# Softmax attention's scores, maximum items and masks issued as four column tiles of 32

## The chip, the cores and the metric

The kernel runs on one core of one Trainium2 chip. The metric is the device time of one execution in microseconds (us). Three runs of the kernel before took 1463.82, 1464.60 and 1467.52 us; the median is 1464.6 us.

## What is computed

Four layers run one after the other on an input `x` of shape (4, 1024, 128), each followed by `x = layernorm(x + layer(x))`: softmax attention, a gated feed-forward layer with ternary weights, linear attention with decay, and a mixture of experts. The change is in the first. It has 16 heads of 8 dimensions:

```
q, k, v = split(x @ w_qkv)                     # per head: 1024 x 8
scores  = q @ k.T / sqrt(8), keys after the query masked with -inf
out     = softmax(scores) @ v
return concat(out) @ w_out
```

## The kernel before

**Units.** A unit is one batch entry and four heads; there are 16 (`NU`). The program of each engine is written out for units 0 and 1, loops over units 2 to 13 with two units in the loop's body (`with_loop(eng, 1, NU // 2 - 1, ...)`, six passes), and is written out again for units 14 and 15. Engines meet by semaphores alone, and each executes its program in the order written.

**The inputs of a product.** q and k are split into three bf16 parts each, which are stacked along the partitions in `sq` and `sk`: 96 rows (`MROW`) give the scores of a query and a key, and three more rows (`PARTS`) in `sq` hold the negated maximum of each query, against rows of ones in `sk`.

**Two passes over the scores.** TensorE first computes the maxima's scores: `item(u, p, k)` writes 128 queries x up to 512 keys for two or four heads into one of two pairs of PSUM banks (`pair[k % 2]`), at line 1206, and adds the causal mask to its last 128 columns with a product of the identity and `mask_qk`, at line 1209. VectorE reduces every item to one maximum per query and head (`top`, line 1367). There are 21 items a unit, numbered 0 to 20, 80 matmuls with their 32 masks. An item waits for the reduction of the item two before it (`s_itc`). When all are reduced, `chain` on VectorE splits the maxima into three parts, `turn_max` on TensorE transposes them (line 1220, eight matmuls with 12 columns of weights), VectorE copies them out (line 1394), and DMAs write them to `sq`.

The second pass, `scores` (line 1231), writes keys x queries with the maximum already taken off, in 36 steps of one bank each (48 matmuls), into three banks in turn. ScalarE takes the exponential of each (line 1320) into one of 12 slots of `pe_`; GpSimd zeroes the triangle above the diagonal in the blocks on it (`triangle`, line 1488).

**The products with v** (`times_v`, line 1256) come in ten groups a unit (`GROUPS`, numbered 0 to 9), after the exponentials (and triangles) of the group are there. They are float32 with 32 columns of weights (8 dimensions, a one for the sum, padding), one head per group of 32 partitions of `pv_bank`: four matmuls that differ in the columns of the array that they use. The profile shows two records for each, one for each pass of a float32 product. VectorE then transposes and normalises (`norm`, lines 1402 to 1414).

**The order on TensorE.** Unit u interleaves its own scores and products with the items of unit u + 1: for each group g, two steps of scores, an item, two steps, an item, then the products of group g - 1, then what is left of the items (`PER_GROUP`). `turn_max(u + 1)` comes after group 7. The items 0 to 2 of unit u + 2 come in group 9. The items of unit 0 are done ahead of all, and unit 15 has none beside it.

Of the kernel before, what the change touches and what calls it, by code (L numbers as in the profile page):

```python
# [21 lines left out]
P = 128  # L22
# [10 lines left out]
PARTS = 3  # L33
SROWS = PARTS * PARTS * D0
MROW = 96
# [76 lines left out]
def program(nc, a, out):  # L112
    with ExitStack() as ctx:
        def sb(name, shape, dt=F32):
            return ctx.enter_context(nc.sbuf_tensor(name, shape, dt))
# [14 lines left out]
        identb = sb("identb", [P, P], BF16)  # L130
        mask_qk = sb("mask_qk", [P, P], BF16)
# [30 lines left out]
        sq = [view([P, HQ, T], BF16) for p in range(2)]  # L162
        sk = [view([P, HQ, T], BF16) for p in range(2)]
# [1004 lines left out]
        def _(e):  # L1168
# [21 lines left out]
            e.wait_ge(s_r1, 4 * B)  # L1190
            e.wait_ge(s_v, 2 * B)

            def item(u, p, k, i=None):

                qt, hs, k0, n = ITEMS[k]
                if k == 0:
                    e.wait_ge(s_st[p][0], 16 * 8 * (i + 1))
                if k == HALF_ITEM:
                    e.wait_ge(s_st[p][1], 16 * 8 * (i + 1))
                if not (isinstance(u, int) and u == 0 and k < 2):  # L1200
                    e.wait_ge(s_itc, NI * u + k - 1)
                for at, h in enumerate(hs):
                    col = at * n if len(hs) == 4 else at * 512
                    dst = pair[k % 2].rearrange("p a c -> p (a c)")[:, col:col + n]
                    diag = k0 + n > qt * P
                    ins = nc.tensor.matmul(dst, sq[p][0:MROW, h, qt * P:(qt + 1) * P], sk[p][0:MROW, h, k0:k0 + n],  # L1206
                                           start=True, stop=not diag, skip_group_check=True)
                    if diag:
                        ins = nc.tensor.matmul(dst[:, n - P:n], identb[:, :], mask_qk[:, :],  # L1209
                                               start=False, stop=True, skip_group_check=True)  # L1210
                ins.then_inc(s_it, 1)

            def turn_max(u):
# [10 lines left out]
            def scores(u, p, steps):  # L1224

                for s in steps:
                    if not (isinstance(u, int) and u == 0 and s < NBANK):
                        e.wait_ge(s_exp, NS * u + s - NBANK + 1)
                    bank = score[s % NBANK]
                    for h, kt, q0, n, at in STEPS[s]:  # L1230
                        ins = nc.tensor.matmul(bank[:, at:at + n], sk[p][0:MROW + PARTS, h, kt * P:(kt + 1) * P],  # L1231
                                               sq[p][0:MROW + PARTS, h, q0:q0 + n], start=True, stop=True,
                                               skip_group_check=True)
                    ins.then_inc(s_qk, 1)

            def times_v(u, p, g):
# [27 lines left out]
            for k in range(NI - 1):  # L1264
                item(0, 0, k, 0)
            turn_max(0)

            def unit(u, p, first, last, i):

                for g in range(NG):  # L1270
                    if g == 0:
                        e.wait_ge(s_mrow, 16 * HQ * (u + 1))
                    steps = range(FIRST_STEP[g], FIRST_STEP[g] + len(GROUPS[g][1]))
                    items = max_work(g, first, isinstance(u, int) and u == NU - 2, last)

                    def next_item():
                        ahead, k = items.pop(0)
                        item(u + ahead, p if ahead == 2 else 1 - p, k, i + 1 if ahead == 2 else i + p)
                    for n in range(2):
                        scores(u, p, steps[2 * n:2 * n + 2])  # L1280
                        if items:
                            next_item()
                    if g or not first:
                        times_v(*((u, p, g - 1) if g else (u - 1, 1 - p, NG - 1)))
                    while items:
                        next_item()
                    if not last and g == CHAIN_SLOT:
                        turn_max(u + 1)
# [300 lines left out]
```

## Time and profile before

| | |
|---|---|
| median of the runs | 1464.6 us |
| the profiled execution: its own time, its span | 1472.18 us, 1470.5 us |
| PE (TensorE matmul), busy in the span | 1281.0 us, 87%, 10608 records |
| PEld (weight loads) | 738.8 us, 10609 records |
| DVE (VectorE) | 979.5 us, 67% |
| ACT (ScalarE) | 642.1 us, 44% |
| POOL (GpSimd) | 536.1 us, 36% |
| mean granted TensorE clock | 0.944 |

The profile is one execution; its terms are compared with its own time, and the median is that of other executions. "Busy" is the time in which at least one instruction of the engine is under way; matmuls overlap one another, and their ends are modelled, so differences between starts say more than durations. The softmax attention's two passes run from 43.8 us (first item) to 579.2 us (last product with v) after the span's start; the scores start at 76.1 us. Records of LDWEIGHTS (PEld) and MATMUL (PE) are separate; every matmul of the program has both.

### The profile page before, as it was taken

To read this page: it belongs to the slowest core of one execution; us is meant where nothing else is said; L and a number is where in the kernel's file an instruction comes from. 1 tells how busy PE (TensorE), PEld (TensorE's weight loads), DVE (VectorE), ACT (ScalarE), POOL (GpSimd) and SP (SyncE) were. 2 spreads that over 40 slices of the span, in tenths; PEclk is the share of its full clock that TensorE was granted. 3 is DMA by queue.
4 is the path that set the end of the run, shared out by engine and by line. 5 is a ranking of instruction groups with operands and counts; after the bars stand their busy time and mean duration, and the time that the engine had idled before them with its cause. 6 is when DMAs were issued, how large, how long until landed. Compare 5 with 4: busy or idle time off the path is not lost. (4 is left out here: it accounts for less than half of the span.)

```text
span 1470.5 us, 33772 instructions
## 1 busy us (share of the span) xinstructions
PE 1281.0 (87%) x10608; PEld 738.8 (50%) x10609; DVE 979.5 (67%) x2119; ACT 642.1 (44%) x1280; POOL 536.1 (36%) x615
## 2 busy tenths in 40 slices
PE   6699999999999996799999999999999977299990
PEld 4233333334333332356556565746565645299980
DVE  6868888877888881247584848485857556366656
ACT  4155556565556655242433334242524231155553
POOL 7112232323232322005261616253444434244456
PEclk9589999999999999799999999999999988599995
DMA  6452111111111110321121303030303050232215
GB/s 190 114 179 54 38 39 36 45 46 48 41 38 36 37 39 21 100 54 40 46 67 30 82 27 86 14 98 14 98 12 87 2 156 2 73 96 65 65 55 173
DMA packets 91756, 93.59 MB, mean 64 GB/s; under 512 B 16816, under 2 KB 77104, under 8 KB 91568
## 3 DMA queue, kind: packets, MB, share of 16 engines
q1 hardware_dynamic: 73872, 74.91, 18.7%
q0 software_dynamic: 9184, 13.39, 3.1%
q10 hardware_dynamic: 8640, 4.53, 1.1%
q8 instruction: 33, 0.54, 0.2%
q14 instruction: 27, 0.22, 0.1%
HBM read 49.84 MB, written 22.63 MB: 49 GB/s over the span
## 5 line engine op out<-in xcount | busy, mean ns | idle before, releaser
L1320 ACT ACTIVATE arena<-banks 128x512 f32<-128x512 f32 x576 | 302.4, 600 | 231.9 <-PE banks L1231 231.3
L1367 DVE TENSOR_REDUCE arena<-banks 128x4 f32<-128x512 f32 (+3 forms) x336 | 347.7, 1057 | 77.3 <-PE banks L1209 71.9
L1206 PE MATMUL banks<-arena 96*128 96x512 bf16 (+3 forms) x768 | 207.8, 344 | 25.7 <-DVE arena L1367 19.0
L424 PE MATMUL banks<-arena,h 128*128 128x512 f32 x512 | 226.7, 593 | 2.4 <-DVEq L369 1.0
L1231 PE MATMUL banks<-arena 99*128 99x512 bf16 (+3 forms) x768 | 176.7, 330 | 16.3 <-ACT arena L1320 11.3
L1488 POOL TENSOR_SCALAR_AFFINE_SELECT arena<-arena 128x512 f32<-128x512 f32 x128 | 79.9, 636 | 241.5 <-ACT arena L1320 241.4
L1256 PE MATMUL banks<-arena 128*32 128x512 f32 (+3 forms) x1536 | 156.8, 496 | 4.4 <-POOL arena L1488 2.7
L424 PEld LDWEIGHTS banks<-arena,h 128*128 128x128 f32 x512 | 94.7, 190 | 110.0 <-issue 105.0
L570 ACT ACTIVATE arena<-banks,sh 128x512 f32<-128x512 f32 x64 | 44.0, 687 | 214.4 <-PE banks L424 214.4
L1206 PEld LDWEIGHTS banks<-arena 96*128 96x128 bf16 x768 | 71.6, 101 | 125.8 <-DVE arena L1367 82.9
L440 POOL TENSOR_TENSOR arena<-arena 128x4 f32<-128x4 f32 x24 | 24.4, 1019 | 278.1 <-DVE arena L438 278.1
L1231 PEld LDWEIGHTS banks<-arena 99*128 99x128 bf16 x768 | 60.2, 98 | 123.2 <-ACT arena L1320 88.7
L1496 POOL DMA_DIRECT2D att_t<-arena x124 | 62.5, 506 | 142.2 <-DVE arena L1414 131.3
L609 POOL TENSOR_TENSOR arena<-arena,qdec 128x512 f32<-128x512 f32 x64 | 87.6, 1391 | 64.1 <-DVE arena L513 42.8
L950 ACT ACTIVATE arena<-banks,b_in 128x128 f32<-128x128 f32 x288 | 82.2, 368 | 63.4 <-PE banks L932 60.2
L983 POOL DMA_INDIRECT best<-arena x72 | 71.8, 998 | 89.2 <-DVE arena L970 48.2
L1209 PE MATMUL banks<-mask_qk,identb 128*128 128x128 bf16 x512 | 102.8, 228 | 0.0
L558 POOL TENSOR_TENSOR arena<-arena,kdec 128x512 f32<-128x512 f32 x64 | 84.5, 1345 | 35.7 <-ACT arena L549 20.7
L684 DVE SCALAR_TENSOR_TENSOR arena<-arena,bdec,banks 128x128 f32<-128x128 f32 x256 | 69.0, 343 | 30.5 <-PE banks L671 30.5
L424 PE MATMUL banks<-h,arena 128*128 x576 | 81.0, 284 | 3.5 <-ACT arena L950 2.4
L932 PE MATMUL banks<-arena 128*128 128x128 f32 x576 | 79.4, 282 | 1.7 <-DVE arena L963 1.7
L823 POOL DMA_INDIRECT rows<-arena x64 | 62.7, 979 | 49.5 <-DVE arena L797 22.6
(162 smaller groups left out, 1947.9 us busy)
## 6 DMA issues: line engine op xcount, KB each, us to landing
arena<-arena SPq DMA_DIRECT2D x160, 128.0 KB, 2.3
arena<-k_parts SPq DMA_DIRECT2D x96, 96.0 KB
arena<-rows SPq DMA_DIRECT2D x72, 65.0 KB
arena<-q_parts SPq DMA_DIRECT2D x64, 64.0 KB
arena<-best SPq DMA_DIRECT2D x16, 256.0 KB, 4.6
k_parts<-arena SPq DMA_DIRECT2D x24, 128.0 KB, 3.0
arena<-q_parts SPq DMA_DIRECT2D x32, 96.0 KB
q_parts<-arena POOLq DMA_DIRECT2D x18, 128.0 KB, 3.0
```

What stands on the lines that cost most here:

```text
L424: ins = nc.tensor.matmul(dst, l, r, start=(n == 0), stop=(n == len(pairs) - 1), skip_group_check=True)
L558: lambda: nc.gpsimd.tensor_tensor(v_dec[:, n % 2, kp, :, :].rearrange("p g (i d) -> p g i d", i=4), v_nat[:, n, 2 * kp:2 * kp + 2, :].rear ...
L609: lambda: nc.gpsimd.tensor_tensor(q_dec[:, n % 2, 4 * kp:4 * kp + 4, :, :], q_all[:, 4 * kp:4 * kp + 4, n * P:(n + 1) * P].rearrange("p i ...
L932: ins = nc.tensor.matmul(banks[:, 2 + k % 2, m * P:(m + 1) * P], w_now[:, k % 4, m * P:(m + 1) * P], x_gT[:, k % 4, :], start=True, stop=T ...
L950: ins = nc.scalar.activation(h_g[:, k % 2, m * P:(m + 1) * P], banks[:, 2 + k % 2, m * P:(m + 1) * P], ACT.Gelu, bias=b_in[:, bass.ds(x, 1 ...
L1206: ins = nc.tensor.matmul(dst, sq[p][0:MROW, h, qt * P:(qt + 1) * P], sk[p][0:MROW, h, k0:k0 + n], start=True, stop=not diag, skip_group_ch ...
L1209: ins = nc.tensor.matmul(dst[:, n - P:n], identb[:, :], mask_qk[:, :], start=False, stop=True, skip_group_check=True)
L1231: ins = nc.tensor.matmul(bank[:, at:at + n], sk[p][0:MROW + PARTS, h, kt * P:(kt + 1) * P], sq[p][0:MROW + PARTS, h, q0:q0 + n], start=Tru ...
L1256: done.append(nc.tensor.matmul(pv_bank[32 * h:32 * h + 32, lo:lo + n], va[p][:, kt, h, :], pe_[:, s % NSLOT, at:at + n], start=(g in (0, 3 ...
L1320: nc.scalar.activation(pe_[:, s % NSLOT, :], score[s % NBANK], ACT.Exp, scale=SCALE0)\
L1367: nc.vector.tensor_reduce(mx[:, 1 if k0 else 0, qt, hs[0]:hs[-1] + 1], src, AX.X, ALU.max)\
L1488: ins = nc.gpsimd.affine_select(out=v, in_=v, compare_op=ALU.is_ge, fill=0.0, base=0, pattern=[[0, v.shape[1]], [1, P]], channel_multiplie ...
```

## The change

Each matmul of line 1206 (items), line 1209 (masks) and line 1231 (scores) had 128 columns of weights and wrote 128 partitions. It becomes four matmuls, one after the other, with 32 columns of the weights each, the same streamed operand, and 32 partitions of the output each. The semaphore is incremented by the last of the four. Nothing else changes: the order of the work, the waits, the banks, the other engines' programs and the transposes of `turn_max` stay.

```diff
+            def columns4(dst, lhs, rhs, start, stop):
+
+                for c in range(0, P, 32):
+                    ins = nc.tensor.matmul(dst[c:c + 32, :], lhs[:, c:c + 32], rhs, start=start, stop=stop,
+                                           skip_group_check=True)
+                return ins
+
             def item(u, p, k, i=None):
...
-                    ins = nc.tensor.matmul(dst, sq[p][0:MROW, h, qt * P:(qt + 1) * P], sk[p][0:MROW, h, k0:k0 + n],
-                                           start=True, stop=not diag, skip_group_check=True)
+                    ins = columns4(dst, sq[p][0:MROW, h, qt * P:(qt + 1) * P], sk[p][0:MROW, h, k0:k0 + n],
+                                   True, not diag)
                     if diag:
-                        ins = nc.tensor.matmul(dst[:, n - P:n], identb[:, :], mask_qk[:, :],
-                                               start=False, stop=True, skip_group_check=True)
+                        ins = columns4(dst[:, n - P:n], identb, mask_qk[:, :], False, True)
                 ins.then_inc(s_it, 1)
...
                     for h, kt, q0, n, at in STEPS[s]:
-                        ins = nc.tensor.matmul(bank[:, at:at + n], sk[p][0:MROW + PARTS, h, kt * P:(kt + 1) * P],
-                                               sq[p][0:MROW + PARTS, h, q0:q0 + n], start=True, stop=True,
-                                               skip_group_check=True)
+                        ins = columns4(bank[:, at:at + n], sk[p][0:MROW + PARTS, h, kt * P:(kt + 1) * P],
+                                       sq[p][0:MROW + PARTS, h, q0:q0 + n], True, True)
                     ins.then_inc(s_qk, 1)
```

## Rows read from the trace of the kernel before

**Rows 1.** Busy time and records of each engine in two units; columns as named.

```profile
core 0: us, PE busy (x) PEld busy (x) DVE busy (x) ACT busy (x) POOL busy (x), PEclk, DMA share, GB/s
...
139.00:202.00 63.00, 58.73 (x463) 24.25 (x462) 51.57 (x71) 37.61 (x72) 18.88 (x34) 1.00 0.18 44
```

**Rows 2.** Timeline of DVE; start, length, what, [idle before <-releaser].

```profile
441.66 2.36 DVE L1367 TENSOR_REDUCE arena<-banks 128x4 f32<-128x1024 f32 x2 [0.46 <-PE banks L1209]
...
452.47 1.23 DVE L1367 TENSOR_REDUCE arena<-banks 128x2 f32<-128x1024 f32 x1 [0.35 <-PE banks L1209]
...
455.73 0.68 DVE L1394 COPY arena<-banks 12x1024 bf16<-12x1024 bf16 x1 [0.87 <-PE banks L1220]
459.13 1.29 DVE L1367 TENSOR_REDUCE arena<-banks 128x4 f32<-128x512 f32 x2 [2.72 <-PE banks L1209]
461.10 0.69 DVE L1367 TENSOR_REDUCE arena<-banks 128x2 f32<-128x512 f32 x1 [0.68 <-PE banks L1209]
461.98 1.92 DVE L1367 TENSOR_REDUCE arena<-banks 128x2 f32<-128x768 f32 x2 [0.19 <-PE banks L1209]
```

**Rows 3.** Timeline of PE around three groups of products with v.

```profile
407.64 1.07 PE L1256 MATMUL banks<-arena 128*32 128x384 f32 x16
408.65 0.60 PE L1231 MATMUL banks<-arena 99*128 99x512 bf16 x2
...
410.73 0.64 PE L1256 MATMUL banks<-arena 128*32 128x256 f32 x8
411.30 0.60 PE L1231 MATMUL banks<-arena 99*128 99x512 bf16 x2
...
413.00 0.22 PE L1209 MATMUL banks<-mask_qk,identb 128*128 128x128 bf16 x1
413.15 1.07 PE L1256 MATMUL banks<-arena 128*32 128x512 f32 x8
414.15 0.60 PE L1231 MATMUL banks<-arena 99*128 99x512 bf16 x2
```

**Rows 4.** Timeline of PE from the transposes of the maxima to the next unit.

```profile
423.30 0.61 PE L1220 MATMUL banks<-identb,arena 128*12 128x128 bf16 x8 [0.18 <-DVE arena L1384]
423.84 0.83 PE L1231 MATMUL banks<-arena 99*128 99x384 bf16 x6
...
426.76 0.22 PE L1206 MATMUL banks<-arena 96*128 96x128 bf16 x1
426.82 0.22 PE L1209 MATMUL banks<-mask_qk,identb 128*128 128x128 bf16 x1
...
427.85 1.07 PE L1256 MATMUL banks<-arena 128*32 128x384 f32 x16
...
429.20 0.59 PE L1231 MATMUL banks<-arena 99*128 99x512 bf16 x2
```

**Rows 5.** Timeline of PE in unit 15, which has no items beside it.

```profile
568.34 1.06 PE L1256 MATMUL banks<-arena 128*32 128x512 f32 x8
...
570.74 1.07 PE L1256 MATMUL banks<-arena 128*32 128x512 f32 x8
```

**Rows 6.** Timeline of PE, the window from 413.14 to 413.17 us alone.

```profile
413.15 0.64 PE L1256 MATMUL banks<-arena 128*32 128x512 f32 x4
```

**Rows 7.** DMA by queue: 139 to 202 us, all queues of 202 to 515, 582 to 720; an issue of the page.

```profile
q8 instruction: 4, 0.07, 0.5%
...
q1 hardware_dynamic: 13039, 11.49, 13.1%
q0 software_dynamic: 2502, 1.29, 2.0%
...
q8 instruction: 7, 0.11, 0.3%
...
arena<-arena SPq DMA_DIRECT2D x160, 128.0 KB, 2.3
```

**Rows 8.** Timeline of PE in the linear attention.

```profile
681.26 1.11 PE L671 MATMUL banks<-arena 64*64 64x64 f32 x64
682.19 1.05 PE L621 MATMUL banks<-arena 64*64 64x256 f32 x16
```

## The prediction

> **What bounds the kernel now.** The change touches only TensorE's program in the softmax attention, so I read the stretches of that part first, by the table of windows. In two whole units (63 us) PE is busy for 58.7 us, DVE for 51.6, ACT for 37.6 [rows 1]. PE is the fullest, but a busy PE contains modelled ends, and 51.6 of 63 is no idle DVE either. So next I read DVE's timeline over one unit, some 31.5 us [rows 2]. DVE has work back to back except in six places, where it waits for TensorE: 0.46, 0.35, 0.87, 2.72, 0.68 and 0.19 us, 5.3 us in all. Between them DVE sets the pace: whatever PE gains there, PE waits longer for DVE. The reader is to see here that a faster PE shortens a unit only by what it takes out of these six gaps.
>
> **What a switch of tile shape costs.** Third, PE's own timeline. The last mask before a group of products with v starts at 413.00 and the products at 413.15 [rows 3]; a mask of 128 columns otherwise takes 0.06 us (426.76 to 426.82 [rows 4]). So going in costs 0.09 us. For the way out I compare groups of two lengths [rows 3]: the groups x16 (384 and then 128 columns) and x8 of 512 columns, each in two passes, last 1.01 and 1.00 us until the next score starts, the group of 256 columns 0.57 us. Half the columns, 0.43 us less: so 0.86 us is streaming and about 0.14 us is fixed. It is paid once, however many rounds of four tiles there are (four in x16, two in x8), so the rounds themselves add nothing. I read it as waiting for the array to empty (some 0.09 again) and the first 32-column weights, that nothing covers. That it is the shape and not bf16 against float32 is seen at turn_max: eight 12-column transposes in bf16 take 0.54 us until a full-width bf16 score starts (423.30 to 423.84 [rows 4]), where eight of 128 columns would be 0.06 x 8 = 0.44 by the masks' pace: 0.09 or 0.10 again, with no change of type.
>
> **The change, part by part.** Removed: per unit 10 groups x (0.09 + 0.14) = 2.3 us, and about 0.2 at the transposes: 2.5 us of PE time, 40 us in 16 units, the most that the change could bring if PE alone were the bound. The parts that lie in DVE's gaps:
> 1. Gap before items 0 and 2, 3 (2.72, 0.68, 0.19): PE's path runs from the transposes over the scores of group 8 and the products of groups 7 and 8. The products of group 8 start at 427.85 [rows 4] although PE has nothing else to do by then: they wait for GpSimd's triangle, which comes from an exponential of group 8, and this moves only by the 0.09 after the transposes. So of this path the 0.09 and the 0.09 to 0.1 behind group 8 remain: 0.18 us, in 14 units: 2.5 us. (What is won at group 7 is lost again in the wait for the triangle.)
> 2. Gap before item 12 (0.46): it hangs on item 11, which DVE itself released, and one group of products in between: 0.23 less 0.03 for the weights and the stagger below: 0.2 us, in 15 units: 3.0 us.
> 3. Gap before item 20 (0.35): from item 12 on PE runs nearly without a wait through four groups of products, 4 x 0.23 = 0.9 us, more than the gap: it closes, 0.35 x 15 = 5.2 us. The rest becomes PE's wait for DVE.
> 4. Gap before the copy of the transposed maxima (0.87): chain of DVE's own results; nothing.
> 5. After the last item (unit 14's end and unit 15) PE and ACT take turns: four scores and a group of products each 2.40 us (568.34 to 570.74 [rows 5]), of which the two switches are 0.2; 13 groups, some waiting for the triangle: I take 2.3 us.
> Sum of the gain: 2.5 + 3.0 + 5.2 + 2.3 = 13.0 us.
>
> Added: every matmul of scores, items and masks becomes four with 32 columns of weights. Four tiles side by side start within one window of 0.03 us [rows 6], so the last ends about 0.02 us after the first. A round costs one matmul's streaming, if its weights load under the round before. In a stream nothing is added. Where PE comes out of a wait, the last tile's semaphore is 0.02 later and the first weights are seen: 0.04 us. In the gaps above that is already off; the 20 items of unit 0 ahead of the loop, where nothing switches, give a loss: 20 x 0.04 = 0.8 us.
>
> Also added: instructions. A unit has 128 matmuls that become 512, so 768 more records with their weight loads, on (463 + 462) / 2 = 463 now [rows 1]. The loop body holds two units. While it is first run, 4 instruction packets of queue q8 arrive for 925 records (I take q8 for PE's: no other engine has so many instructions); from 202 to 515 us there is none: the body stays in PE's instruction memory [rows 7]. Afterwards the body is 925 + 1536 = 2461 records, at 925 / 4 = 231 a packet and with the uncounted register instructions staying as they are, 10 to 11 packets. The most that this trace shows to stay is the later loop's, 7 packets fetched between 582 and 720 [rows 7]. So 10 may not stay. Fetched in order they are harmless: one per 6 us. But at each of the 5 jumps back to the top (6 passes) the top may be missing. Price of one: from nothing (it stays, or PE's queue covers it) to 2.3 us, what a small transfer of this kernel takes from issue to landing (the 128 KB moves in [rows 7]). PE's sequencer is at the jump when the triangle lets group 8 go, at 427.85, and the next unit's scores start at 429.20 [rows 4], 1.3 us later. What shows is 2.3 - 1.3 = 1.0 at the upper end; I take 0.8 us, 5 x 0.8 = 4 us, bounds 0 and 5 x 2.3 = 11.5 us.
>
> The Trainium skill speaks to this place ("Runtime: NRT & Kernel Launch", section "Instruction fetch mechanics"): PE's instruction memory holds 2048 instructions in blocks of 256, and a taken branch to a block that isn't there stalls for a fetch. The rows agree as far as they go (231 counted records a packet, no fetch during the small loop); none shows a stall. By it the body would be over the limit and the 4 us would be sure to be paid at least in part; without it they could be nothing.
>
> Sum: -13.0 + 0.8 + 4 = -8.2 us. The profiled execution took 1472.2 us for a span of 1470.5, 7.6 us above the median of 1464.6; the terms are differences, so I take them from the median: 1456.4.
>
> **Rivals.**
> A. The body stays or the jumps are covered, and PE's gain reaches DVE a little more than I count: 1464.6 - 13 = 1452, down to 1447 where group 7's gain counts as well (0.2 x 14 = 3 us). For it: the six gaps are all PE's. Against it: packets.
> B. Jumps cost double (two packets at each, or 2.3 us all exposed): 11.5 us instead of 4, total -0.7: 1464, no change. For it: nothing covers PE at this place, DVE is idle there too. Against it: PE's queue holds some work.
> C. Slower: a round of four bf16 tiles doesn't keep a full-width matmul's pace, because the weights of 32 columns don't hide. Place: each of 128 rounds a unit. The nearest row: the fixed part at the products has 0.03 us more at its start than one switch. At 0.027 a round, 3.5 us a unit against 2.5 won; in the stretches that end in DVE's gaps lie about 90 rounds, 2.4 us against the 0.73 won there, less what the DVE-bound waits swallow, about 1 us a unit: 15 us, 1480. It decides from about 10 ns a round. Against it: four rounds cost no more overhead than two [rows 3], and 16 rounds of four 64-column float32 tiles take 0.93 us (681.26 to 682.19 [rows 8]), 0.058 a round against 0.054 of streaming (0.43 us for twice 256 columns, scaled to 64): 4 ns more, with a change of operands in it. For it: no row has bf16 tiles at the short rounds of 128 columns, where eight instructions must issue in 0.055 us.
> The Trainium skill speaks for C ("TensorEngine Tiling (Array Packing)", "Performance Considerations" and "Restrictions"): column tiling excludes the fast weight load. Whether the slower loads hide under a 128-column bf16 round no row shows. By this rule alone the time would go towards 1480.
> D. The switch isn't what the 0.09 is (say, each group waits so for its semaphore in any case): nothing is won, the added costs stay: 1464.6 + 4.8 = 1469. Against it: the same 0.09 at the transposes.
>
> **How the numbers follow.** No change that this kernel's measurement can tell is within 0.3%, 4.4 us: 1460.2 to 1469.0. Forecast (1452 to 1460) 0.45; A 0.18; B 0.18; C 0.13; D 0.06. Faster: 0.45 + 0.18 = 0.63; same: most of B and half of D, 0.20; slower: C, part of B and D, 0.17. A range of 1447 to 1467 leaves out C, a part of D, and gains beyond A.
>
> **What will show it.** PE's timeline: the next score starts 0.86 us after a group x8 of 512 columns began, not 1.00; a round of four 512-column tiles takes 0.216 us, one of 128 columns 0.056 (C: 0.08 or more). DVE's gap before item 20 gone, that before item 12 near 0.25, the 0.87 as it was, a unit near 30.8 us. In the DMA view instruction packets between 202 and 515 us, about 10 per 62 us if the body doesn't stay, and every second unit a PE gap of about a microsecond after item 2, with the cause "issue". The prediction is wrong if rounds are slower than full-width matmuls, if the jump costs 2 us or more in the open, or if DVE's gaps stay as they are.

## The result and the profile after

The changed kernel takes 1475.45 us (median of four runs, 1474.34 to 1478.62); the kernel before took 1464.21 us beside it. The ratio is 1.0076, 95% interval 1.0053 to 1.0099: slower by 11 us, where 8 us faster was forecast. The profiled execution took 1478.62 us, the longest of the four, and has a span of 1477.0 us.

I read the same views as before. First the windows of PE and DVE: the two units ahead of the first jump, and then the 250 us in which four of the jumps lie (the columns are those of [rows 1]).

```profile
139.00:202.00 63.00, 57.22 (x1300) 29.46 (x1292) 52.14 (x71) 39.42 (x75) 19.99 (x36) 1.00 0.18 46
202.00:265.00 63.00, 54.68 (x1123) 26.78 (x1124) 50.64 (x69) 34.80 (x67) 17.21 (x33) 0.95 0.16 45
265.00:515.00 250.00, 217.28 (x4564) 110.01 (x4566) 188.62 (x255) 139.17 (x264) 68.90 (x124) 0.93 0.16 43
```

In the first two units DVE has more to do in 63 us than in [rows 1] (52.1 against 51.6) and PE, with 1300 records for 463, is busy for 1.5 us less: the work runs faster. From 202 us on both are busy for less, and the granted clock is below 1. So the loss isn't in the column tiles; it begins with the loop's second pass. The pace of a unit, further down, says the same.

DVE's timeline over one unit without a jump, the rows that answer to [rows 2]:

```profile
437.50 0.68 DVE L1399 COPY arena<-banks 12x1024 bf16<-12x1024 bf16 x1 [0.87 <-PE banks L1226]
440.60 1.29 DVE L1372 TENSOR_REDUCE arena<-banks 128x4 f32<-128x512 f32 x2 [2.42 <-PE banks L1196]
442.69 0.69 DVE L1372 TENSOR_REDUCE arena<-banks 128x2 f32<-128x512 f32 x1 [0.80 <-PE banks L1196]
443.56 1.84 DVE L1372 TENSOR_REDUCE arena<-banks 128x2 f32<-128x768 f32 x2 [0.19 <-PE banks L1196]
...
454.75 2.35 DVE L1372 TENSOR_REDUCE arena<-banks 128x4 f32<-128x1024 f32 x2 [0.23 <-PE banks L1196]
```

2.72 became 2.42, 0.68 became 0.80, 0.46 became 0.23, the 0.87 is as it was; the 0.35 ahead of item 20 is gone.

PE's timeline around products with v and over the jump, the rows that answer to [rows 3] and [rows 4]:

```profile
401.90 1.03 PE L1261 MATMUL banks<-arena 128*32 128x512 f32 x8
402.77 0.67 PE L1196 MATMUL banks<-arena 99*32 99x256 bf16 x20
...
404.53 1.07 PE L1261 MATMUL banks<-arena 128*32 128x384 f32 x16 [0.35 <-POOL arena L1493]
405.42 0.29 PE L1196 MATMUL banks<-arena 96*32 96x256 bf16 x4
405.53 0.24 PE L1196 MATMUL banks<-mask_qk,identb 128*32 128x128 bf16 x4
405.59 0.29 PE L1196 MATMUL banks<-arena 96*32 96x256 bf16 x4
405.70 0.24 PE L1196 MATMUL banks<-mask_qk,identb 128*32 128x128 bf16 x4
409.08 0.78 PE L1196 MATMUL banks<-arena 99*32 99x512 bf16 x12 [3.14 <-issue]
...
412.22 0.51 PE L1196 MATMUL banks<-arena 96*32 96x384 bf16 x4 [1.55 <-issue]
```

The next score starts 0.87 us after a group x8 of 512 columns (1.00 before), and a round of four tiles takes 0.11 us with 256 columns (405.42 to 405.53) and 0.06 with 128 (405.53 to 405.59), the pace of full width (0.06 by [rows 4]; 365.06 to 365.17 us with 256 columns in full_straight, a kernel of the next section): those steps of the prediction hold. But at 405.9, after item 2 and ahead of the next unit's first score, where the loop jumps to its top, PE stops for 3.14 us. The first jump's stop, at 203.5, is 3.37 us long. Both are far over the 0.8 us that I took and over the 2.3 us of my bound. After it PE runs at half the clock (the same columns as above; 0.51 is the mean of the two levels, almost all at 1.2 GHz):

```profile
206.00:212.90 6.90, 5.88 (x80) 2.69 (x84) 2.67 (x4) 2.17 (x4) 0.64 (x1) 0.51 0.12 35
410.70:417.60 6.90, 5.38 (x80) 2.82 (x84) 4.41 (x6) 1.86 (x5) 0.63 (x1) 0.51 0.01 2
437.00:451.00 14.00, 12.33 (x335) 7.10 (x332) 10.09 (x14) 7.70 (x15) 4.16 (x8) 1.00 0.19 52
```

The DMA queues, 139 to 202 us and then 202 to 515 us, answer to [rows 7]:

```profile
q8 instruction: 11, 0.18, 1.2%
...
q8 instruction: 56, 0.92, 1.3%
```

11 packets in the loop's first pass, and 12 in each pass after it (56 in 313 us, of which a pass takes 67): the body doesn't stay in PE's instruction memory.

The same queue tells what each stop at a jump consists of. At 405.94 PE stops; a packet of 16 KB starts at 406.02 and ends at 407.48; PE goes on at 409.08. So it is at all five jumps: the packet starts 0.08 to 0.27 us after PE has stopped and takes 0.9 to 1.6 us, and PE goes on 1.6 to 1.7 us after its end. Ahead of the second stop, of 1.55 us, a packet ends at 410.83, and PE goes on at 412.22, 1.4 us later. (These are the starts and durations of the trace's q8 packets.)

For the pace of a unit I use a row of DVE's chain that occurs once a unit (the CAST of `chain`), asked from 190 to 500 us: its count, and its first and last start. Before, then after:

```profile
L1382 DVE CAST arena<-arena x10: 197/199/199, 200.6 to 486.2; 128x32 bf16<-128x32 f32 x10
```

```profile
L1387 DVE CAST arena<-arena x9: 195/195/195, 197.1 to 466.8; 128x32 bf16<-128x32 f32 x9
```

Before, (486.2 - 200.6) / 9 = 31.73 us a unit. After, a unit without a jump takes 30.6 (197.1 less 166.5, the start of the one ahead), and one with a jump 35.9 to 36.7. One unit without a jump took 31.9. There PE waited for a DMA, and the granted clock was 0.50 from 380.0 to 383.4 us:

```profile
379.49 2.29 PE L1196 MATMUL banks<-arena 96*32 96x512 bf16 x32 [1.41 <-DMA arena<-q_parts]
```

### The profile page after: what moved, and what is told of

Read it like the earlier page. It is cut to its first block and busy times, and to the rows that moved or that the text cites. A ratio compares the mean times of both kernels' runs of the same rounds, so it can differ in the third digit from the quotient of the medians.

```text
span 1477.0 us, 46060 instructions
## 1 busy us (share of the span) xinstructions
PE 1265.1 (86%) x16752; PEld 773.2 (52%) x16753; DVE 974.2 (66%) x2119; ACT 644.3 (44%) x1280; POOL 532.3 (36%) x615
## 3 DMA queue, kind: packets, MB, share of 16 engines
q1 hardware_dynamic: 73872, 74.91, 18.4%
## 5 line engine op out<-in xcount | busy, mean ns | idle before, releaser
L1196 PE MATMUL banks<-arena 99*32 99x512 bf16 (+7 forms) x6144 | 357.6, 344 | 62.3 <-issue 17.5
L1196 PEld LDWEIGHTS banks<-arena 96*32 96x32 bf16 (+1 forms) x6144 | 159.8, 99 | 238.1 <-DVE arena L1372 71.4
L1196 PE MATMUL banks<-mask_qk,identb 128*32 128x128 bf16 x2048 | 110.4, 234 | 0.2
L558 POOL TENSOR_TENSOR arena<-arena,kdec 128x512 f32<-128x512 f32 x64 | 80.9, 1290 | 30.1 <-PE banks L546 25.8
L680 ACT COPY arena<-banks 128x512 f32<-128x512 f32 x64 | 34.4, 590 | 89.7 <-PE banks L671 89.7
L932 PEld LDWEIGHTS banks<-arena 128*128 128x128 f32 x576 | 71.5, 195 | 2.5 <-issue 2.3
```

Of the source, the lines that this page charges most:

```text
L558: lambda: nc.gpsimd.tensor_tensor(v_dec[:, n % 2, kp, :, :].rearrange("p g (i d) -> p g i d", i=4), v_nat[:, n, 2 * kp:2 * kp + 2, :].rear ...
L932: ins = nc.tensor.matmul(banks[:, 2 + k % 2, m * P:(m + 1) * P], w_now[:, k % 4, m * P:(m + 1) * P], x_gT[:, k % 4, :], start=True, stop=T ...
L1196: ins = nc.tensor.matmul(dst[c:c + 32, :], lhs[:, c:c + 32], rhs, start=start, stop=stop, skip_group_check=True)
```

## The experiments

Twelve runs follow, in four groups. Each group has its own runs of the kernel before, to which its ratios refer: 1464.33 us for the first four kernels, 1468.29 for the next three, 1471.11 for pause_54, pause_20, straight_again and after_again, 1468.33 for pause_31. Between groups it is the ratios that compare, not the medians.

**The loop taken away, with and without column tiles.** In TensorE's program alone all 16 units are written out, so that nothing jumps back. The same edit in both kernels; `full` is the kernel before, `cols` the changed one.

```diff
-            units(e, unit)
+            for u in range(NU):
+                unit(u, u % 2, u == 0, u == NU - 1, u // 2)
```

> The changed kernel (all in four column tiles) with TensorE's attention program written out for all 16 units, no loop; the other engines keep their loops. Theory J (the loss is the 5 jumps back to the top of a body that no longer stays in TensorE's instruction memory, each 3.1 + 1.6 us of stall and a half clock after it): a unit of the changed kernel without a jump repeats in 30.6 us, one with a jump in 36.7, so 5 x 6.1 = 30 us come back: 1475.4 - 30 = 1445 us, 0.987 of the kernel before. Rival R (the four-tile rounds or the number of instructions are the cost, wherever they are): written out, the same instructions run, 1475 us; a straight program even fetches more packets.

> The kernel before (full-width matmuls) with TensorE's attention program written out in the same way; its waits then compare with constants, without register instructions. Theory J: its body of two units stayed in memory, its jumps cost nothing: 1464 us, ratio 1.000. Rival W (any loop or the register instructions at the waits cost TensorE time): faster, by as much as a good part of what the written-out changed kernel wins, 1450 or less.

cols_straight took 1448.34 us, ratio 0.989 (0.9868 to 0.991), full_straight 1463.94 us, 0.9997 (0.9985 to 1.0008). Their chain rows, cols_straight first:

```profile
L1388 DVE CAST arena<-arena x10: 195/195/197, 195.5 to 470.8; 128x32 bf16<-128x32 f32 x10
```

```profile
L1383 DVE CAST arena<-arena x10: 196/198/199, 200.5 to 485.5; 128x32 bf16<-128x32 f32 x10
```

30.59 and 31.67 us a unit. The column tiles bring 16 us, and all that the changed kernel loses, 27 us between ratios 1.0076 and 0.989, comes with the loop. That the waits now compare with constants gains nothing by itself: full_straight has that too. Nor is it the fetching as such: cols_straight fetches 49 packets from 202 to 515 us, about as many as the changed kernel's 56, but in order, and hides all of them.

**Half as many jumps.** The loop's body holds four units, with two jumps instead of five. At full width the body then holds 2 x 925 = 1850 counted records, where two units of column tiles have 2461 by the prediction's count.

```diff
-            units(e, unit)
+            for u in range(2):
+                unit(u, u % 2, u == 0, False, 0)
+            with_loop(e, 0, (NU // 2 - 2) // 2,
+                      lambda j: [unit(2 * (2 * j + m) + p, p, False, False, 2 * j + m)
+                                 for m in range(1, 3) for p in range(2)])
+            for u in range(NU - 2, NU):
+                unit(u, u % 2, False, u == NU - 1, u // 2)
```

> The kernel before (full-width matmuls) with four units in TensorE's loop body instead of two: 3 passes, 2 jumps. Twice the 4 packets and more of the two-unit body, so about as many as didn't stay in the changed kernel. Theory J: the long body doesn't stay, 2 jumps of 5 to 6 us each, though not one matmul is tiled: 1464 + 11 = 1475 us, instruction packets all through the attention, two half-clock stretches. Rival R (tiles are the cost): 1464 us.

> The changed kernel with four units in TensorE's loop body: 3 passes, 2 jumps instead of 5. Theory J: three jumps fewer, 1475.4 - 3 x 6.1 = 1457 us. Rival R: 1475 us.

full_4units took 1475.1 us, ratio 1.0075 (1.0058 to 1.0092): with no column tile in it the kernel before becomes as slow as the changed one, by two jumps. In the table of PE's waits, 200 to 480 us (total, times, longest):

```profile
PE banks L1231 <- issue: 6.1, 2, 3.1
```

The kernel before has no such row. The two units with a jump took 37.3 and 36.5 us, 5.5 and 4.8 over the others, for stops of 3.0 and 3.1. The body of four full-width units, too, is fetched anew (23 packets from 202 to 515 us, 10 of them in the pass between the two jumps, where the kernel before has none): 1850 counted records, with the uncounted ones beside them, are already more than stays.

cols_4units took 1465.13 us, 0.9998 (0.9983 to 1.0012). Three jumps fewer won back 10 us against the changed kernel's 1475.45, where 18 were expected (1457 us). Its two jumps don't account for the whole distance to cols_straight, (1465.13 - 1448.34) / 2 = 8.4 us each: by the trace each is 6.5 to 6.7 us (37.1 and 37.2 us for 30.5 and 30.6). Most of the rest, 0.1 to 0.9 us a unit, lies in units without a jump. In five of them PE stops, again with the cause "issue", for 0.17 to 0.62 us, 1.8 us in all, and each time it goes on 1.3 to 1.6 us after the end of a 16 KB packet, as after the changed kernel's second stop. So here fetching in order is not always hidden; 2 us more in those units have no row.

**One of the two groups of matmuls alone, no loop.** `wide` issues one full-width matmul. In cols_items_only the scores stay full width, in cols_scores_only the items and masks do.

```diff
-                        ins = columns4(bank[:, at:at + n], sk[p]...
+                        ins = wide(bank[:, at:at + n], sk[p]...
```

> Written out like cols_straight, but only items and masks in four column tiles; the scores go back to full width. Theory S (the gain is the switches of tile shape that go away): the order of a unit has 20 changes between full width and 32 columns in the kernel before, none with all in tiles, and 32 here, since the scores now stand between items and products. The 20 were worth 16 us (1464 to 1448), 0.05 us each; 12 more than before at 0.05 to 0.1 us, 15 units: 1473 to 1482 us, slower than both. Rival T (the tiled matmuls are themselves quicker, by their weight loads or their concurrency): most matmuls are tiled, so most of the gain stays, about 1454 us.

> Written out, only the scores in four column tiles, items and masks at full width. Theory S: 36 changes of shape a unit, 16 more than before: 1476 to 1488 us. Rival T: a third of the tiled matmuls, a third of the gain, about 1459 us.

They took 1482.45 us, ratio 1.0102 (1.0075 to 1.0128), and 1488.72 us, 1.0143 (1.0116 to 1.017), each less than 1 us over its expected range, beside a kernel before that was itself 4 us slower than in the first group. Chain rows in this order:

```profile
L1392 DVE CAST arena<-arena x10: 197/197/197, 205.3 to 497.2; 128x32 bf16<-128x32 f32 x10
```

```profile
L1392 DVE CAST arena<-arena x9: 195/195/198, 205.5 to 467.6; 128x32 bf16<-128x32 f32 x9
```

32.43 and 32.76 us a unit. Half the change makes the kernel slower although no round is slower, since scores and items alternate: counted in the traces, TensorE's tile shape changes 0 times a unit in cols_straight, 20 in full_straight, 32 and 36 here. The units take 30.59, 31.67, 32.43 and 32.76: over cols_straight 0.054, 0.058 and 0.060 us a change. On PE's own timeline a change takes more. First cols_items_only, where two full-width scores of 512 columns stand between items in tiles, all bf16, then full_straight, where nothing changes:

```profile
373.91 0.60 PE L1202 MATMUL banks<-arena 99*128 99x512 bf16 x2
374.45 0.35 PE L1196 MATMUL banks<-arena 96*32 96x384 bf16 x4
```

```profile
365.23 0.59 PE L1231 MATMUL banks<-arena 99*128 99x512 bf16 x2
365.67 0.33 PE L1206 MATMUL banks<-arena 96*128 96x384 bf16 x1
```

0.54 us for 0.44: the change takes 0.10 us of PE, and a unit pays a little over half of it, since much of PE's time lies under DVE's. The number of changes orders all four kernels, and that is what the whole change wins; whether each kind of change costs exactly the same isn't shown.

**The blocks shifted.** 90 increments of an unused semaphore at the start of PE's program move every later instruction against the blocks in which the memory is filled. The second stop after a jump (1.55 us above) would be a block's edge soon behind the jump's target.

```diff
+            for _pad in range(90):
+                e.sem_inc(s_hold, 1)
```

> The changed kernel with its loop of two units (5 jumps), and 90 semaphore increments that nobody waits for at the very start of TensorE's program, while it waits for its inputs. They move the loop's top by 90 instructions, from near the end of a fetched block (TensorE stops a second time some 75 instructions after the top) to near the start of the next. Theory J2 (the first stall is the fetch of the block with the top, the second is the fetch of the block after it, which begins only when the first is there): the second stall (1.6 us) goes, the half clock after it gets shorter, 5 x 2 = 10 us: 1465 us. Rival K (each jump costs its 6 us wherever the top lies, for instance because the clock falls): 1475 us.

It took 1487.83 us, 1.0131 (1.0103 to 1.0159): by the ratios 8 us more, not 10 less, than the changed kernel. The increments themselves were hidden only in part: they take 13.6 us of PE's sequencer at the start, 0.151 us each, and the first product with v starts at 95.1 us for 87.2, 7.9 us later. The row of PE's sequencer (number, then first and last start):

```profile
L1170 PEldq EVENT_SEMAPHORE  x90: 51/51/51, 1.0 to 14.6; - x90
```

From there on the trace gains on the changed kernel's: its 15 units from the first chain to the last take 490.2 us for 493.8. At the jumps there is one stop now, but 3.2 to 3.7 us long:

```profile
PE banks L1198 <- issue: 13.7, 4, 3.7
```

The five units with a jump took 35.2 to 36.5 us, on average 36.0 instead of 36.4. The expected 2 us a jump did not come: it is 0.4. The expectation took a second stop at every jump, but the changed kernel has it at one of five (at two of five when it ran again, below), and the first stop is longer here instead (13.7 / 4 = 3.4 us a jump, as much as the changed kernel's 16.5 / 5 = 3.3 with both). That no second stop shows at five jumps fits the idea that it hangs on where the blocks lie, but with so few it isn't shown. And stops of 3.3 to 3.4 us don't explain a price of 5.5 to 5.8. So I looked at the half clock.

**A stop without a missing packet.** cols_straight with N increments ahead of units 4, 6, 8, 10 and 12, where the changed kernel jumps. All packets still come in order.

```diff
             for u in range(NU):
+                if u in (4, 6, 8, 10, 12):
+                    for _pad in range(N):
+                        e.sem_inc(s_hold, 1)
                 unit(u, u % 2, u == 0, u == NU - 1, u // 2)
```

> cols_straight (all tiles, no loop in TensorE's attention) with 54 semaphore increments that nobody waits for, before units 4, 6, 8, 10 and 12: the five places of the jumps. 90 of them took 7.9 us in cols_shifted, so 54 take 4.8 us, which is how long after group 8's products the next unit's scores started at a jump. No packet is missing here. Theory J3 (a jump costs what any stop of TensorE of 3.4 us at this place costs: the 3.4, and a half clock after it, 5.3 to 6 us in all; fetching itself has no further price): 1448.3 + 5 x 5.5 = 1476 us, half clock after each stop. Rival F (the fetch costs more than the stop, through slower issue or DMA after the jump): 1448.3 + 5 x 3.4 = 1465 us.

> The same with 20 increments, 1.8 us. Theory Q (TensorE's queue covers 1.3 us at this place, as predicted): about 0.5 us of stop remain, clock stays up: 1448.3 + 5 x 0.5 = 1451 us. Rival: nothing is covered, 1448.3 + 5 x 1.8 = 1457 us.

> The version with no loop, as pause_54 and pause_20, with 31 increments ahead of units 4, 6, 8, 10 and 12: at the 0.151 us that they stood apart there, 4.7 us of PE's sequencer, of which some 0.8 us were covered in pause_20. So PE should stop for 3.1 to 3.9 us at five places, as long as it stops at a jump of the changed kernel, with every instruction packet fetched in order. Theory (a stop brings half the clock after it, and that is the rest of a jump's price beside the missing packets): each place costs the stop and 1.3 to 2 us more, 5.0 to 5.9 us in all, so 25 to 30 us over the version without increments, beside a jump's 5.3 to 6.1. Rival (a bare stop costs itself, and the second stop behind a jump is the missing next packet's alone): 3.1 to 3.9 a place, 16 to 20 us in all, and no half clock after it.

Beside the first two of them the two kernels to be compared ran once more:

> cols_straight again on this chip, to stand beside the two runs with pauses: 1448 us by its first runs.

> The changed kernel again on this chip, to stand beside the runs with pauses: 1475 us by its first runs.

| kernel | median us | ratio (95%) | a stop, us | each place costs, us |
|---|---|---|---|---|
| straight_again | 1453.01 | 0.9887 (0.9856 to 0.9919) | none | |
| pause_20 | 1468.57 | 1.0 (0.9984 to 1.0016) | 2.2 | 3.3 |
| pause_31 | 1480.77 | 1.0083 (1.0067 to 1.01) | 3.9 | 5.8 |
| after_again (five jumps) | 1482.69 | 1.0097 (1.0065 to 1.0129) | 3.7 | 5.8 |
| pause_54 | 1500.47 | 1.0217 (1.0185 to 1.025) | 7.5 | 9.4 |

The kernels that ran again took 5 and 7 us more than in their first group, as the kernel before did, and their ratios are the same within the intervals. A stop is the total of the row "issue" in PE's waits from 200 to 480 us by the number of places in that window (both stops of a jump together for after_again, 18.4 / 5). A place costs what the units with it took over the others, on average. The rows are these; pause_20, pause_31, pause_54 (four of its places lie in the window), and that of the changed kernel's first profile:

```profile
PE banks L1196 <- issue: 10.9, 5, 2.2
```

```profile
PE banks L1196 <- issue: 19.4, 5, 4.0
```

```profile
PE banks L1196 <- issue: 29.8, 4, 7.6
```

```profile
PE banks L1196 <- issue: 16.5, 6, 3.4
```

Two expectations failed. pause_54 was to take 1476 us and took 1500: I had taken 7.9 / 90 = 0.088 us for an increment from cols_shifted, where 5.7 of the 13.6 us were hidden, but they stand 0.151 us apart, there as here, so that it stopped for 7.5 us, not as long as a jump. pause_20 was to take 1451, or 1457 if nothing is covered, and took 1469: it stopped for 2.2 us instead of 0.5 to 1.8, and half clock followed at four of its five places. pause_31 has the right length, and it is also the price of a jump. Its timeline of PE at one place, and the window behind another:

```profile
405.45 1.12 PE L1196 MATMUL banks<-arena 99*32 99x512 bf16 x12 [3.88 <-issue]
```

```profile
204.40:211.30 6.90, 6.70 (x97) 3.62 (x101) 3.67 (x4) 2.17 (x4) 0.64 (x1) 0.51 0.01 2
```

A stop of 3.9 us that has nothing to do with fetching brings the same half clock (at four of the five places the last packet had ended 3 us or more before PE went on, at one 1.65 us). By its chain rows the five places cost (498.5 - 194.3) - (470.8 - 195.5) = 28.9 us:

```profile
L1391 DVE CAST arena<-arena x10: 196/196/197, 194.3 to 498.5; 128x32 bf16<-128x32 f32 x10
```

So 5.8 us each, 3.9 of it the stop and 1.9 what follows it, which the trace shows as PE at 1.2 GHz for 3.4 us at two places (they cost 5.2 and 5.5 us) and for 6.8 us at three (6.2 each). The rival, that a bare stop costs itself alone, gives 19 us and falls. Within pause_31 the places with 3.4 us of half clock cost 1.3 and 1.6 us beyond their stop, those with 6.8 us 2.3. Where in pause_20 the clock stayed full after the stop (one of five places), that place cost 2.4 us, close to the stop's 2.2; the four with half clock behind them cost 3.2 to 3.8.

## Why the prediction was wrong

**The failed step** is the price of the jump: "What shows is 2.3 - 1.3 = 1.0 at the upper end; I take 0.8 us, 5 x 0.8 = 4 us, bounds 0 and 5 x 2.3 = 11.5 us." The mechanism came as told in its first half: the body didn't stay, 11 to 12 packets a pass, and a gap with the cause "issue" after item 2. Its size was wrong by a factor of seven, and the truth lay outside the bounds: 27 us between the ratios of the changed kernel and cols_straight, 29.7 us between the medians of after_again and straight_again, 5.4 to 5.9 a jump. Three things in it:

- The fetch. I took 2.3 us for it, from data transfers [rows 7], less 1.3 us for what lies ahead in PE's queue, and so expected a stop of about 1 us. The five first stops are 2.7 to 3.4 us: longer than the transfer with no cover taken off. The packets say why: nothing of the transfer lay under PE's work, since the packet started only once PE had stopped (0.08 to 0.27 us later), and to its 0.9 to 1.6 us come 1.6 to 1.7 us from its end until PE goes on. What the sequencer does ahead of the packet's start no run shows.
- In some jumps (one in five in the profiled execution) a second stop of 1.55 us follows. Its packet had ended 1.4 us before PE went on, which fits a next block that isn't there either. Rival B said "two packets at each, or 2.3 us all exposed": both at once and more.
- After the stop the clock is halved, for 6.8 to 10.2 us. No term and no rival had this. It is 1.9 us a place in pause_31; in the changed kernel the five jumps cost 5 x 5.8 = 29 us, of which 16.5 are stops, so that 12.5 lie behind them, 2.5 a jump. That all of the 2.5 is the clock isn't shown: 6.8 us of half clock were worth 2.3 in pause_31.

The prediction's own sign of being wrong came, "if the jump costs 2 us or more in the open". Rival B (the jumps cost double) had the right side and not the size: 11.5 us at most. What came was B's bound two and a half times over.

**The gain was in the right places and a little larger.** Forecast 13.0 us; by the ratios 0.9997 and 0.989 it is 15.7 us. DVE's groups of reductions, idle time before them in 12 units (busy and mean, then idle), full_straight and then cols_straight:

```profile
L1368 DVE TENSOR_REDUCE arena<-banks 128x2 f32<-128x1024 f32 x145 | 172.4, 1203 | 7.6 <-PE banks L1209 4.6
...
L1368 DVE TENSOR_REDUCE arena<-banks 128x2 f32<-128x512 f32 x24 | 16.5, 686 | 8.2 <-PE banks L1209 8.2
L1368 DVE TENSOR_REDUCE arena<-banks 128x4 f32<-128x512 f32 x24 | 16.4, 682 | 32.6 <-PE banks L1209 32.6
L1368 DVE TENSOR_REDUCE arena<-banks 128x4 f32<-128x1024 f32 x12 | 14.7, 1224 | 5.5 <-PE banks L1209 5.5
```

```profile
L1373 DVE TENSOR_REDUCE arena<-banks 128x2 f32<-128x1024 f32 x144 | 170.0, 1199 | 1.6
...
L1373 DVE TENSOR_REDUCE arena<-banks 128x2 f32<-128x512 f32 x24 | 16.5, 686 | 9.6 <-PE banks L1196 9.6
L1373 DVE TENSOR_REDUCE arena<-banks 128x4 f32<-128x512 f32 x24 | 16.4, 682 | 29.1 <-PE banks L1196 29.1
L1373 DVE TENSOR_REDUCE arena<-banks 128x4 f32<-128x1024 f32 x12 | 14.7, 1224 | 2.7 <-PE banks L1196 2.7
```

- Gaps before items 0, 2 and 3: (32.6 - 29.1 + 8.2 - 9.6) / 12 = 0.175 us a unit, 0.18 forecast. As told, what is won at group 7 is lost in the wait for the triangle (still 0.35 us at 404.53 above).
- Gap before item 12: (5.5 - 2.7) / 12 = 0.23, 0.2 forecast.
- The reductions of 1024 elements, item 20 among them: (7.6 - 1.6) / 12 = 0.50, 0.35 forecast. Term 3 was too small: beside the gap that I listed, PE's gain also closes small idle pieces among the others.
- The copy's gap: no gain from the tiles (9.5 us in both), as said.
- Together 0.9 us a unit of 31.67 - 30.59 = 1.08; reductions 4 ns shorter, twelve a unit, are 0.05 more. 0.1 us is in no row.
- The removed PE time was counted as 10 groups and the transposes besides. The trace has 20 changes of shape, not 22: the transposes follow a group of products (422.05 and 423.30 us in the kernel before), which already has 32 columns. This touches the upper limit of 40 us alone, no term of the sum.
- The tail: from the last chain to the last product with v 29.7 us became 28.6, 1.1 for 2.3 forecast. A turn of four scores and a group takes 2.19 (554.48 to 556.67 us in cols_straight) for 2.40 [rows 5], as told; fewer turns than I took decide it. In the sum of the gain this shortfall and the excess of term 3 (0.15 x 15 = 2.2 us) partly cancel.
- The start: unit 0's first chain is 1.0 us later (70.8 for 69.8), 0.8 forecast, but between executions of the same kernel it varies by as much (70.9 and 69.3 us in the changed one). From the first chain to the second 36.0 us became 33.2, for which no term stands; much of that may be the clock (half until 87.4 us in full_straight, until 80.6 in cols_straight) and no gain of the tiles, see the last section.

The sum with the measured terms is -15.7 + 27 = +11.3 us, the result; it must be, as both terms are taken from ratios to the same kernel. The traces give the second term independently: the five jumps of the changed kernel cost 28.9 us over its other units.

**Rivals A, C and D.** A asked for covered jumps and falls. C, slower rounds, falls: full width's pace at 128, 256 and 512 columns (0.06, 0.11 and 0.21 us, the last from 376.11 to 376.32 in the changed kernel), and cols_straight is the fastest kernel. The Trainium skill ("TensorEngine Tiling (Array Packing)", section "Restrictions") says that column tiling disables the fast weight load, which spoke for C. No cost of it shows here: with 1292 weight loads in 63 us where there were 462, a 128-column round of four bf16 tiles still takes 0.06 us. D falls by cols_straight itself and by the two half changes. The Trainium skill's "Runtime: NRT & Kernel Launch", "Instruction fetch mechanics", says that a taken branch to a block that isn't there stalls, and the traces agree: 2.7 to 4.3 us at each such jump. Its limit of 2048 instructions, in blocks of 256, is eight blocks; the traces agree as far as they go, with a loop of 7 packets that stays [rows 7] and bodies of 10 and 12 that don't. I weighed this rule as to whether the price is paid and took the price from a data transfer; that is the error.

## What to carry to other kernels

A change that multiplies instructions is first to be checked against what a loop's body holds: here a body that stays costs nothing at its jumps, one that doesn't costs 4.8 to 6.7 us at each, and the same body written out without a jump costs nothing again, since in order the fetches hide (in cols_straight; in the loop of cols_4units not quite). TensorE's tile shape costs 0.06 us of a unit's time at each change, so it pays to have one shape all through (-16 us) and costs to have it in one half alone (ratios 1.0102 and 1.0143). A stop of TensorE is to be priced at more than itself: one of 3.9 us cost 5.8 here. The version to use is cols_straight: 0.989 of the time before.

## What the runs showed of the hardware

- A jump whose target isn't in PE's instruction memory: 2.7 to 4.3 us of stop (the longest in cols_4units), in bodies of both kinds; a second one of 1.55 us at some. In all 19 of these first stops (changed kernel twice, cols_shifted, full_4units, cols_4units) a 16 KB packet of q8 takes 0.9 to 1.9 us, and PE goes on 1.6 to 1.9 us after its end.
- After a stop of 3.9 us with full clock and work on either side, 3.4 or 6.8 us at 1.2 GHz; of five stops of 2.2 us four had it (3.4 us), one hadn't. A wait of 1.41 us for a DMA had it too (the changed kernel at 379.49).
- A semaphore increment by PE's program took 151 ns in a row of 90 at the start and in rows of 20 to 54 between the units; of a row of 20, 0.8 us is hidden by what PE has queued (20 x 0.151 - 2.2).
- A change of tile shape takes 0.10 us of PE between bf16 and bf16 (cols_items_only), and costs a unit of this kernel 0.054 to 0.060 us.
- The same program's first unit, from the first chain to the second, took 36.0 us in full_straight and 33.9 in full_4units, though the two are the same up to there. The clock differs: half until 87.4 us in the one, full from 79.5 in the other. It is 2 us that a single trace can put in the wrong account. full_straight, then full_4units:

```profile
79.50:87.50 8.00, 7.65 (x32) 3.68 (x31) 6.49 (x7) 1.78 (x5) 0.64 (x1) 0.50 0.93 334
79.50:87.50 8.00, 6.99 (x52) 3.13 (x51) 7.88 (x9) 2.34 (x5) 1.86 (x3) 1.00 0.93 344
```
